# A decoder layer on one core: a shared down projection in rounded parts, a second buffer for x1, the choice of experts ahead of the moments, and a subtraction moved to GpSimd

## The reference

```python
x = layernorm(x + mamba(x))                       # with its own norm, conv, scan, gate, residual
q, k, v = xpos(x @ Wq), xpos_inverse(ctx @ Wk), ctx @ Wv
x = layernorm(x + ((q @ k.T) * decay_mask) @ v)
shared = (silu(x @ shared_gate.T) * (x @ shared_up.T)) @ shared_down.T
probs = sigmoid(x @ router_w.T + routing_bias)    # 8 experts
scores, indices = top_k(probs, 2)                 # scores divided by their sum
routed = sum over the 2 chosen of score * ((silu(x @ gate_w[e]) * (x @ up_w[e])) @ down_w[e])
x = layernorm(x + shared + routed)                # all in float32
```

## Time and profile before

| | |
|---|---|
| time, median of 3 runs | 1850.27 us (1849.88, 1850.27, 1854.23) |
| the profiled execution | 1854.46 us, of which span 1852.8 us |
| mean granted clock of TensorE | 0.963 |
| busy over the span | PE 1686.3 us (91%), PEld 1435.5 (77%), DVE 1183.4 (64%), ACT 807.0 (44%), POOL 720.3 (39%) |
| `down` of the shared expert | L2384, 512 records, 115.5 us busy |
| `rest_c` | L1936, 16 operations, 32.8 us busy |
| stage of attention and shared expert | about 550 to 1134 us |

### The profile page before, as it was taken

How to read it: one execution, slowest core, us unless ns; L and a number is a source line. 1 busy time by engine, 2 the same in 40 slices (tenths; PEclk the granted TensorE clock), 3 DMA queues, 4 the chain that set the end, 5 groups by cost and what they waited for, 6 DMA issues and landing times.

```text
span 1852.8 us, 35774 instructions
## 1 busy us (share of the span) xinstructions
PE 1686.3 (91%) x9652; PEld 1435.5 (77%) x9653; DVE 1183.4 (64%) x2682; ACT 807.0 (44%) x1507; POOL 720.3 (39%) x625
## 2 busy tenths in 40 slices
PE   6999968999947999999999997999999999999980
...
GB/s 140 180 197 201 154 260 149 248 248 248 230 114 129 70 94 81 81 104 78 72 104 81 80 161 133 53 58 53 58 53 58 53 56 55 56 55 53 58 44 362
DMA packets 137705, 220.64 MB, mean 119 GB/s; under 512 B 40544, under 2 KB 110368, under 8 KB 129328
## 3 DMA queue, kind: packets, MB, share of 16 engines
...
## 4 chain that ended last, share of the span: by engine, by line
PE 38%; DMA 16%; issue 6%; DVE 4%; POOL 3%; ACT 2%; SPq 0%; POOLq 0%; ACTq 0%; another core or an unknown queue 0%; DVEq 0%
DMA acc<-back_y,back_token 14%; PE back_ps L2482 10%; PE back_ps L2384 5%; PE back_ps L2502 5%; PE back_ps L2370 4%; PE back_ps L2361 3%; PE back_ps L2280 2%; POOL back_turned_qk L1733 2%; PE back_ps L2315 2%; ACT back_out L1901 2%; PE back_ps L2323 2%; PE back_ps L2491 1%; DVE back_y L2237 1%; PE back_ps L2302 1%; PE back_ps L2268 1%
## 5 line engine op out<-in xcount | busy, mean ns | idle before, releaser
L2482 PE MATMUL back_ps<-back_w_gu,back_xe_T 128*128 x1620 | 413.0, 404 | 1.5 <-DVE back_xe_T L2218 1.5
L1764 POOL DMA_INDIRECT acc<-back_y,back_token x135 | 209.2, 1549 | 461.5 <-DVE back_y L2237 364.2
L2482 PEld LDWEIGHTS back_ps<-back_w_gu,back_xe_T 128*128 128x128 f32 x1620 | 297.4, 189 | 61.6 <-issue 2.4
L2502 PE MATMUL back_ps<-back_w_down,back_he_T 128*128 x1620 | 225.3, 288 | 1.5 <-DVE back_he_T L2230 1.5
L2502 PEld LDWEIGHTS back_ps<-back_w_down,back_he_T 128*128 128x128 f32 x1620 | 200.7, 188 | 1.8 <-issue 1.7
L1183 PE MATMUL front_ps<-front_xn_T,front_w_in_parts 128*128 128x512 f32 x768 | 187.7, 401 | 5.2 <-issue 3.3
L1721 POOL DMA_INDIRECT sorted<-back_x,back_slot x128 | 136.7, 1068 | 135.1 <-DVE back_slot L2050 100.8
L1183 PEld LDWEIGHTS front_ps<-front_xn_T,front_w_in_parts 128*128 128x128 f32 x768 | 144.3, 191 | 42.1 <-issue 6.3
L2226 DVE TENSOR_TENSOR back_h<-back_h,back_ps 128x512 f32<-128x512 f32 x135 | 92.9, 688 | 121.3 <-PE back_ps L2482 121.3
L1014 DVE SCALAR_TENSOR_TENSOR front_conv<-front_ps,front_conv_wb,front_conv 128x508 f32<-128x508 f32 (+2 forms) x192 | 140.8, 740 | 43.7 <-ACT front_conv L844 38.0
L1895 ACT ACTIVATE back_he_T<-back_ps 128x512 fp32r<-128x512 f32 x135 | 80.8, 599 | 199.9 <-PE back_ps L2491 199.9
...
## 6 DMA issues: line engine op xcount, KB each, us to landing
back_xe<-sorted SPq DMA_DIRECT2D x135, 136.0 KB, 2.5
...
front_c_rep<-c_parts SPq DMA_DIRECT2D x128, 64.0 KB, 4.2
...
```

Of the source, the lines that this page charges most:

```text
L1764: pool.indirect_dma_start(out=d["acc"][:, :], out_offset=bass.IndirectOffsetOnAxis(ap=token[:, r:r + 1], axis=0), in_=y[:, r % 2], in_offs ...
L2482: op = nc.tensor.matmul(dst[:, r % 2], xe_T[:, x_part, k], w_gu[:, bass.ds(e, 1), m, w_part, k], start=(n == 0), stop=(n == len(PASSES) - 1))
L2502: op = nc.tensor.matmul(ps_y[:, 0:D_MODEL], he_T[:, h_part, k], w_down[:, bass.ds(e, 1), w_part, k], start=(n == 0), stop=(n == len(DOWN_P ...
```

## The change

- **Down projection in parts.** `h_T` holds two chunks only and takes the place of `silu_T`: Silu writes into it, `hidden` multiplies in place. ScalarE rounds each chunk to `h_high` (`round_h`), VectorE computes `h_low` (`rest_h`). The weights `w_down_s` are split the same way, once, in step 0. `down` runs over the four chunks, three matmuls for each sequence and chunk, 48 in place of 16 f32 ones.
- **x1 in two buffers.** Its load no longer waits for the sum of the group in work; it is turned between `score` and chunk 2, rounded on ScalarE behind the sigmoid, its rest computed behind `decay_scores`.
- **Order on VectorE.** `pick` stands between `sum_rows_of` and the rest of h 2; `normalize` stands between `expert_out` and `place_rows`.
- **rest_c on GpSimd**, behind the scatters of the second choice; c's rounding on ScalarE moves behind x1's, and c is loaded when k is projected.
- `base` shares the buffer of `v`, whose copy waits for the store of the base before. Other buffers move; the last loads and splits of the experts' down weights change places. The space for descriptors of the DMAs that GpSimd issues is set to 8192 (it is at its default before), which frees the room for the second x1.

```diff
-        x1 = at("x1", 140, [P, GS, D_MODEL])
-        c_raw = at("c_raw", 144, [P, KM, GT])
-        v = at("v", 148, [P, GS, D_MODEL])
-        scores_T = at("scores_T", 152, [P, GT])
-        sum_rows = at("sum_rows", 154, [P, GS, D_MODEL])
+        x1 = [at("x1_0", 140, [P, GS, D_MODEL]), at("x1_1", -7.75, [P, GS, D_MODEL])]
+        v = base = at("v", 152, [P, GS, D_MODEL])
+        c_raw = at("c_raw", 76, [P, KM, GT])
+        scores_T = at("scores_T", 156, [P, GT])
+        sum_rows = at("sum_rows", 198.75, [P, GS, D_MODEL])
...
-        h_T = at("h_T", 120, [P, KF, GT])
+        h_high = at("h_high", 120, [P, KF, GT], F32R)
+        h_low = at("h_low", 180.5, [P, KF, GT], F32R)
...
-        base = at("base", 180.5, [P, GS, D_MODEL])
-        silu_T = at("silu_T", 184.5, [P, 2, GT])
-        w_down_s = at("w_down_s", 188.5, [P, KF, D_MODEL])
+        h_T = at("h_T", 144, [P, 2, GT])
+        w_down_s = [at("w_down_s_high", 188.5, [P, KF, D_MODEL], F32R), at("w_down_s_low", 148, [P, KF, D_MODEL], F32R)]
+        w_down_s_raw = at("w_down_s_raw", 148, [P, KF, D_MODEL])
...
-                    a = attention[0]
+                    a, ua = attention
                     if not is_at(a, GROUPS - 1):
-                        sp.wait_ge(c_T_ready, a + 1)
+                        if not is_at(a, 0):
+                            sp.wait_ge(sum_ready, 2 * a)
+                        sp.dma_start(x1[1 - ua], d["x1"][a + 1]).then_inc(x1_loaded, 16)
+                        sp.wait_ge(k_done, 2 * (a + 1))
                         sp.dma_start(c_raw, d["ctx_T"][a + 1]).then_inc(c_loaded, 16)
-                        sp.wait_ge(sum_ready, 2 * (a + 1))
-                        sp.dma_start(x1, d["x1"][a + 1]).then_inc(x1_loaded, 16)
...
-                        load_w_down(0, 1, 2, 3)
+                        load_w_down(0, 1, 3)
                         load_chunks(11, 12, 13, 14)
                         sp.wait_ge(scattered[0], 16 * TOP_K * GS * PAIRS)
                         load_w_down(5)
@@ -1668,8 +1674,7 @@
                         sp.wait_ge(chunk_ready, 14)
                         load_w_down(4)
                         sp.wait_ge(down_done, GROUPS)
-                        sp.wait_ge(base_stored, 16 * (GROUPS - 1))
-                        load_w_down(7)
+                        load_w_down(2, 7)
...
+            def rest_c(a):
+                pool.wait_ge(c_high_ready, a + 1)
+                nc.gpsimd.tensor_tensor(c_T[:, 1], c_raw, c_T[:, 0].bitcast(F32), ALU.subtract).then_inc(c_T_ready, 1)
+
+            rest_c(0)
...
                 if expert and not is_at(expert[0], 0):
                     scatter(expert[0] - 1, 1 - expert[1], 1)
+                if attention and not is_at(a, GROUPS - 1):
+                    rest_c(a + 1)
                 if attention:
                     pool.wait_ge(mean_ready, GS * (a + 1))
                     pool.sem_inc(pool_passed, 1)
...
             in_steps(pool, step)
-            for e in (2, 3):
+            for e in (3, 2):
...
+            def round_h(g, i):
+                act.wait_ge(h_ready, KF * g + i + 1)
+                if i == 0 and not is_at(g, 0):
+                    act.wait_ge(down_done, g)
+                nc.scalar.activation(h_high[:, i], h_T[:, i % 2], ACT.Copy).then_inc(h_high_ready, 1)
...
                         act.wait_ge(attended, a)
+                    if not early(a):
+                        act.wait_ge(base_stored, 16 * (a - 1))
                     nc.scalar.activation(v, ps_rows, ACT.Copy).then_inc(v_ready, 1)
...
-                if attention and not is_at(a, GROUPS - 1):
-                    act.wait_ge(k_done, 2 * (a + 1))
-                    round_c(a + 1)
...
+                    if i == 2 and attention and not is_at(a, GROUPS - 1):
+                        round_x1(a + 1)
+                        round_c(a + 1)
                     if expert:
                         act.wait_ge(gate_done, KF * g + i + 1)
                         if i:
-                            act.wait_ge(h_ready, KF * g + i - 1)
-                        nc.scalar.activation(silu_T[:, i % 2], ps_wide[:, (2 * i + 2) % 3], ACT.Silu).then_inc(silu_ready, 1)
+                            act.wait_ge(h_low_ready, KF * g + i - 1)
+                        nc.scalar.activation(h_T[:, i % 2], ps_wide[:, (2 * i + 2) % 3], ACT.Silu).then_inc(silu_ready, 1)
+                        if i:
+                            round_h(g, i - 1)
                     if i == 1 and is_at(expert and g, GROUPS - 1):
                         w_down_high(0)
                         w_down_high(1)
                         chunk_high(11)
+                if expert:
+                    round_h(g, KF - 1)
...
-                    w_down_high(2)
+                    act.wait_ge(base_stored, 16 * (GROUPS - 1))
                     w_down_high(3)
...
                     w_down_high(4)
+                    w_down_high(2)
                     w_down_high(7)
-                if attention and not is_at(a, GROUPS - 1):
-                    round_x1(a + 1)
                 if is_at(attention and a, 0):
                     for name in SPLIT[3:]:
                         high_of(name)
+                    act.wait_ge(w_down_s_loaded, 16)
+                    nc.scalar.activation(w_down_s[0], w_down_s_raw, ACT.Copy).then_inc(w_down_s_high_ready, 1)
...
             def hidden(g, i):
                 dve.wait_ge(up_done, KF * g + i + 1)
                 dve.wait_ge(silu_ready, KF * g + i + 1)
-                if not is_at(g, 0) and i == 0:
-                    dve.wait_ge(down_done, g)
-                nc.vector.tensor_tensor(h_T[:, i], silu_T[:, i % 2], ps_wide[:, 2 * i % 3],
+                nc.vector.tensor_tensor(h_T[:, i % 2], h_T[:, i % 2], ps_wide[:, 2 * i % 3],
                                         ALU.mult).then_inc(h_ready, 1)
+
+            def rest_h(g, i):
+                dve.wait_ge(h_high_ready, KF * g + i + 1)
+                nc.vector.tensor_tensor(h_low[:, i], h_T[:, i % 2], h_high[:, i].bitcast(F32), ALU.subtract
+                                        ).then_inc(h_low_ready, 1)
...
             low_of("W_q", 1)
             rest_x1(0)
-            rest_c(0)
             low_of("W_v", 2)
...
                 if expert:
                     add_bias(g)
-                if attention and not is_at(a, GROUPS - 1):
-                    rest_c(a + 1)
                 if expert:
                     if not attention:
                         chunk_low(10)
@@ -2149,22 +2171,31 @@
                         place_rows(g, u)
                         plan_tiles()
                     hidden(g, 1)
+                    rest_h(g, 0)
                     if not attention:
                         chunk_low(11)
+                last = is_at(attention and a, GROUPS - 1)
                 if attention:
                     decay_scores(a)
+                    if not last:
+                        rest_x1(a + 1)
                 if expert and attention and u:
                     chunk_low((g - 1) // 2)
                 if is_at(expert and g, GROUPS - 2):
                     chunk_low(EARLY)
                 if expert:
                     hidden(g, 2)
+                    rest_h(g, 1)
                     if not attention:
                         place_tiles()
                 if attention:
-                    sum_rows_of(a)
+                    sum_rows_of(a, ua)
                 if expert:
+                    if attention:
+                        pick(g, u)
+                    rest_h(g, 2)
                     hidden(g, 3)
+                    rest_h(g, 3)
                 if attention:
                     stats_of(a)
                 if expert:
@@ -2175,22 +2206,20 @@
                         w_down_low(0)
                         w_down_low(1)
                         chunk_low(14)
-                last = is_at(attention and a, GROUPS - 1)
-                if expert and attention:
-                    pick(g, u)
                 if last:
                     normalize(a, ua)
-                elif attention:
-                    rest_x1(a + 1)
                 if expert:
                     expert_out(g, u)
+                if attention and not last:
+                    normalize(a, ua)
                 if expert and attention:
                     place_rows(g, u)
-                if attention and not last:
-                    normalize(a, ua)
                 if is_at(attention and a, 0):
                     for n, name in enumerate(SPLIT[3:]):
                         low_of(name, 4 + n)
+                    dve.wait_ge(w_down_s_high_ready, 1)
+                    nc.vector.tensor_tensor(w_down_s[1], w_down_s_raw, w_down_s[0].bitcast(F32), ALU.subtract
+                                            ).then_inc(w_down_s_ready, 1)
...
-            def down(g, ahead, first):
-                if is_at(g, 0):
-                    pe.wait_ge(w_down_s_loaded, 16)
-                if first == 0:
```

(34 more changed lines are left out.)

27 lines of the change are left out of this document (14 added, 13 removed).

## The result

The changed kernel takes 1887.34 us (median of 4 runs, 1885.91 to 1890.80); the kernel before took 1850.08 beside it. The ratio is 1.0192, 95% interval 1.0180 to 1.0203: slower by 1.9%, some 36 us, where +24 was forecast. The forecast range ends at 1886 us: by the ratio the time is 1885.8 (1.0192 of 1850.27), the median itself lies 1.3 us above it. The profiled execution took 1890.8 us with a span of 1889.1.

What follows compares the result with a forecast made beforehand. Before, TensorE's own sum and a nearly equal ring over VectorE, GpSimd and TensorE bound the step; after, the ring alone. Steps +24.8, start -4, end +3.3 gave +24: 1874 us as a median, range 1848 to 1886.

Steps and rivals of the forecast that it cites:

- the ring over the slots: Loop through VectorE, GpSimd and TensorE from one score to the next: forecast 35.67 us a step, against 33.90 before.
- S+21.56: S is the start of a step's score matmuls; VectorE's write of the slots was to end 21.56 us later.
- exclusion: A VectorE subtraction of two SBUF tiles and a GpSimd op exclude each other; 0.69 us a step.
- The forecast's own sign: Sign that the forecast is right: score to score 35 to 36 us in the attention and shared-expert stage.
- The 0.69 before sum_rows: VectorE's rest of h 1 waits for GpSimd's rest_c, so sum_rows starts at S+8.2 instead of 7.51.
- the bound of 1.3: Upper bound, in us, for rest_c delaying rest of h 1, when the chunk split pushes rest_c later; lower bound 0.
- the start: Between attend of step 0 and q of step 1, the second x1 buffer saves 4 us, bounds 0 and 8.3.
- The end: Last step: turn of the last x2 2.3 us later, plus 1 for subtractions meeting scatters; together +3.3.
- B: Rival: the ring over the slots without exclusion, +14, 1864 us, or 1858 with the lower scatter value; chance 0.18.
- E: Rival: smaller descriptor space or stored-base wait holds GpSimd or ScalarE 0.8 us a step; +11, 1885 to 1895; chance 0.07.
- D: Rival: TensorE stays the bound, with pick out of the way; step 32.7, -22, 1828 us; chance 0.13.
- TensorE's own sum: TensorE's work in one step: 33.5 us before, less 1.15 from the down projection, 32.4 after.

Runs made afterwards that it cites:

- Run 2: The changed kernel with place_rows ahead of normalize on VectorE again, nothing else; 1849.03 us, ratio 0.9974.
- Run 10: The changed kernel with all eight scatters behind the next step's xpos sums and the rest of ctx between the two groups of four; 1845.12 us, ratio 0.9953.
- Run 1: The changed kernel with seven matmuls whose result nobody reads in TensorE's idle time ahead of up 0; 1874.20 us, ratio 1.0115.
- Run 9: The changed kernel with only the shared down projection back in plain f32; 1860.65 us, ratio 1.0033.
- Run 5: The changed kernel with the first choice's scatters also moved behind the next step's xpos sums, all eight ahead of the rest of ctx; 1876.26 us, ratio 1.0129.
- Run 4: The changed kernel with rank ahead of the projection's third quarter and place_rows between hidden 3 and its rest; 1856.39 us, ratio 1.0008.
- Run 12: Run 10 with the choice of the experts in two parts around hidden 3; 1834.84 us, ratio 0.9883.
- Run 7: Run 2 with the shared down projection in plain f32, without roundings or rests of h; 1839.98 us, ratio 0.9929.
- Run 8: Run 2 with the rest of ctx on VectorE again, behind the rests of x1; 1846.92 us, ratio 0.9968.
- Run 3: The changed kernel with pick behind the statistics again; 1884.47 us, ratio 1.0166.

## Why the prediction was right in its mechanism and short in its size

**The bound and the ring: right.** The forecast had TensorE fall from the bound and the ring over the slots set the step. Run 2 moves only the slots, Run 10 only GpSimd's scatters and the rest of ctx between them; each by itself brings the step from 36.5 to 33.4 or 33.6. The forecast ring was S+21.56 to the slots (20.87 and 0.69 of exclusion) and 14.11 from there to the next score, 35.67. The full-clock step shows 21.53 and 13.88, 35.41; the steps without a chunk split are shorter, 34.97 in Run 1 at full clock. The forecast's own sign, steps of 35 to 36 us, holds for four of the fourteen alone; the mean is 36.51.

**Its terms.** The order was as forecast: pick right behind sum_rows, TensorE waiting for the k parts and for h_low, normalize released by rstd, expert_out at no cost. xpos of k is back at 2.51. The 48 matmuls take 0.120 each. The 0.69 before sum_rows seems the right size in the steps with a chunk split (S+8.17, forecast 8.20), but it is made of two things, one of which was no term. In them rest of h 1 takes 1.18, 0.49 of it beside the rest of ctx. In the other steps it takes 0.74, and sum_rows starts at S+7.74 (825.36 behind the score at 817.62). What is left against Run 9's S+7.39 comes in both kinds from Silu 2, whose table load (822.09) stands behind the roundings of x1 and ctx. Rest of ctx and h 1 together are worth 2.9 us when they meet in full (Run 5): the bound of 1.3 that I gave for this was too small, though this kernel does not reach it.

**The step that failed: the sum took TensorE's matmuls at full clock.** The prediction says that TensorE idles some 3 us a step and prices this at nothing. Ten of fourteen steps then run `up` 0 or gate 1 at 1.2 GHz, which costs 1.6 us in each. Run 1 fills the idle time and the time falls by 14 us, more than the whole gap between the forecast (+24) and the result (+36). A second, small one is the first scatter that comes 1.2 us late in two steps (2.4 us). What was over-counted goes the other way: the ring 0.46 a step (-6.4 us, 35.21 in Run 1 without its two late scatters against 35.67), and the start (5.3 gained, 4 taken).

Checked against the total: 14 x 1.31 (35.21 less 33.90) is 18.4, the low clock 15.7 and the late scatters 2.4: together the +36.5 of the steps.

The end has the right size, 2.2 and 1.0 against 2.3 and 1. The 2.2 is the longer way to normalize, as counted. The 1.0 is luck: it stood for scatters that more subtractions stretch, and the last scatter ends 2.6 us earlier behind the turn of x2 than before (1161.60-1129.96 = 31.64 against 34.19). The first routed tile is loaded 0.3 later all the same, and what makes up the other 0.7 stays open. That the result still falls into the range by its ratio is luck too: the upper end, 1886, was meant for the ring alone, and the low clock used it up.

**The rivals.** B, the ring without exclusion, would have been 1864. Of E, something of the smaller descriptor space may be in the late scatters (see the last section), 2.4 us in all and not 0.8 a step; the wait for the stored base shows only in Run 4. D, TensorE still the bound, was to need the choice out of the way and to give 1828 with steps of 32.7. That was not this kernel, but Run 12 gives its numbers, with the choice still on VectorE and only split around hidden 3: steps of 32.57 and 0.9883 of 1850, which is 1828 us. TensorE's own sum of 32.4 was right.

**Parts of the change, one by one.** Taken back alone, the parts of the projection are worth 29 us in the changed order (Run 9) and, with the slots ahead, some 8 us (Runs 2 and 7, 0.9974 and 0.9929). The move of ctx is worth nothing to 0.1 us a step (Run 8), the place of pick nothing (Run 3), the exchange of normalize and place_rows 40 us (Run 2). These don't add, since in Runs 2, 9 and 10 the low clock, 15.7 us of steps, went together with the longer ring. The new setting of the descriptor space was never taken back. The second buffer of x1 was not undone by itself; the first step, 5.3 us shorter, is what it shows.
